# Cross attention in quarters of the context, with a running maximum

## The chip, the cores and the metric

One Trainium2 chip, one of its cores. The time is the device time of one execution in microseconds (us), median of several runs.

## The reference, cut to what matters

`x` is 8 batches of 128 tokens by 512, `ctx_768` 8 batches of 2048 context rows by 384. Everything is float32.

```python
x = x + xattn(layernorm(x), ctx_768)      # 8 heads of 64: this part is changed
x = x + attn(layernorm(x))                # causal, 128 tokens, softmax over the queries' axis
x = x + ffn(layernorm(x))                 # hidden 2048, 8-bit rounding of hidden and w2

def xattn(x, context):
    q, k, v = heads(x @ Wq), heads(context @ Wk), heads(context @ Wv)
    attn = softmax(einsum('bihd,bjhd->bhij', q, k) * 64 ** -0.5)      # over 2048 context rows
    return einsum('bhij,bjhd->bihd', attn, v) @ Wo + bo
```

## The kernel before, in words

**Split operands.** Almost every product is made of float16 halves: a value is kept as `_h` (its float16 rounding) and `_l` (the float16 of what is left), and `three_passes` (L653 to L659) multiplies high by high, low by high and high by low over the chunks of the contraction (three chunks of 128 for the context).

**Slots.** The cross attention is a loop of 128 slots (`SLOTS`). A slot is one batch, one pair of heads (4 pairs) and one quarter of the context (512 rows). Before, the order is batch, pair, quarter: four slots in a row are one pair's quarters, a stage; the context of a whole batch is held, and two batches of it (`ctx_h`, `ctx_l`). In a slot TensorE (`steady`, L808) makes
- the values of the next slot (`value_tiles`): two row tiles by four heads, 18 products of 256 columns into bank `v_ps`;
- the keys of the pair and quarter (`key_quarter`): 9 products of 512 columns into `k_ps`;
- the weighted values of five slots ago (`weighted_values`, L749 and L752): 16 products of 128 and 64 columns;
- in even slots, the scores of the last two slots (`scores`, L727), 12 products into `e_ps0` and `e_ps1`.

**The other engines** follow in an order that is written out by hand, and wait on semaphores. An engine takes its instructions in this order only, so what waits holds up all behind it.
- ScalarE (`steady`, L1238): in odd slots `quarter_bias` for two slots (the maximum as a bias), `exps` (each head's exponentials twice, as float16 `p_h` and float32 `p_f`, which also give the sums `p_sum`), `v_high` and `k_high` (the high halves out of PSUM), and once a quarter `ctx_high` with the DMA of a later quarter into `raw`.
- VectorE (`steady`, L1605): in odd slots two `quarter_maximum` (L1531), then `accumulate` (the weighted values onto `acc`, times a `fade` that brings the four quarters to one maximum), then `fade_sums`, `add_sums` or `o_reciprocal`, then `v_low`, `stage_low` once in four slots, and `k_low`. `value_tiles` waits for the `v_low` of the tile before it (`v_split`), as there is one bank.
- GpSimd (L2057): `p_low` (L1984, 1024 elements a partition), `o_norm` (four small instructions that turn `acc` into float16 halves), `ctx_low` (L1974, 1536 elements), and near the end `add_bias` and `weight_high` (L2044), with VectorE's `weight_low` behind it.
- SP's queue turns `p_h` and `p_l` by DMA transposes, then finished outputs and weights.

Before, `ctx_low` stands once in four slots, in slot 4n+2, behind `p_low`.

## Time and profile before

| | |
|---|---|
| time, median of 3 runs | 918.98 us (918.54 to 919.09) |
| span of the profiled execution, first to last instruction | 917.6 us |
| TensorE busy | 903.4 us |
| VectorE, ScalarE, GpSimd busy | 590.5, 628.3, 504.8 us |
| granted TensorE clock | full, in all 40 slices |

The profiled execution's own time is not listed beside its span; the median of the runs stands 1.4 us above that span. TensorE's matmuls overlap, so the mean duration of one is longer than its share of the time: what one costs is read from how far a group moves the start of the next. Overlap is also why a group of rows can sum to more than the time it took.

### The profile page before, as it was taken

Reading aid. Unit: us, or ns where it says so; the run is one execution under the profiler, and the core shown is the slowest. Engines: PE = TensorE matmul, PEld = TensorE weight load, DVE = VectorE, ACT = ScalarE, POOL = GpSimd, SP = SyncE. Lnnn points to the kernel's source line nnn. Section 1 sums busy time; section 2 is a strip of 40 time slices with the busy share of each in tenths; the row PEclk is TensorE's granted clock in tenths of the full one; section 3 lists DMA queues with packets and bytes.
Section 4 is the critical chain, followed back from the end, with each engine's and each line's share of the span. In section 5 each row is a group of like instructions: output and inputs, shape, how many; then the busy total and the mean of one; then the engine's idle time right before and its main releaser. Section 6 shows DMA issues by size and latency. Waiting matters only on the chain.

```text
span 917.6 us, 20100 instructions
## 1 busy us (share of the span) xinstructions
PE 903.4 (98%) x7470; PEld 564.5 (62%) x7470; DVE 590.5 (64%) x1069; ACT 628.3 (68%) x1398; POOL 504.8 (55%) x393
## 2 busy tenths in 40 slices
PE   6999999999999999999999999999999999999998
PEld 3556666666666666666666666666666455544444
DVE  6546666656666666666666666666667769886634
ACT  4857887777788788788878778877776523235540
POOL 4637656566556666666665655787777755310000
PEclk9999999999999999999999999999999999999999
DMA  9478677876767677677677868967999662333502
GB/s 333 98 142 167 135 129 141 163 145 139 136 142 131 135 146 138 132 137 141 134 143 152 157 130 140 194 133 146 186 190 165 105 133 64 72 86 74 183 13 80
DMA packets 340271, 126.38 MB, mean 138 GB/s; under 512 B 316113, under 2 KB 317905, under 8 KB 340177
## 3 DMA queue, kind: packets, MB, share of 16 engines
q1 hardware_dynamic: 325232, 96.66, 57.0%
q10 hardware_dynamic: 14944, 28.45, 9.6%
q8 instruction: 61, 1.00, 0.4%
q14 instruction: 34, 0.27, 0.1%
HBM read 45.36 MB, written 2.10 MB: 52 GB/s over the span
## 4 chain that ended last, share of the span: by engine, by line
PE 90%; DVE 3%; ACT 2%; SPq 2%; DMA 1%; issue 1%; ACTq 0%; DVEq 0%
PE v_ps L658 28%; PE k_ps L658 26%; PE e_ps L727 9%; PE e_ps L658 8%; PE o_ps L749 6%; PE o_ps L752 3%; PE e_ps L1014 3%; PE o_ps L1007 1%; PE e_ps L1007 1%; PE o_ps L768 1%; DMA raw<-in_ctx_t 1%; PE o_ps L947 1%; PE v_ps L1007 1%; DVE q_max L1531 1%; SPq L624 1%
## 5 line engine op out<-in xcount | busy, mean ns | idle before, releaser
L1984 POOL TENSOR_TENSOR p_l<-p_f,p_h 128x1024 f16<-128x1024 f32 x128 | 272.4, 2128 | 237.3 <-ACT p_f L1195 237.3
L1190 ACT ACTIVATE p_h<-e_ps,bias 128x512 f16<-128x512 f32 x256 | 175.7, 686 | 2.6 <-issue 0.5
L1195 ACT ACTIVATE p_f<-e_ps,bias 128x512 f32<-128x512 f32 x256 | 176.4, 689 | 0.0
L1526 DVE TENSOR_TENSOR k_l<-k_ps,k_h 128x512 f16<-128x512 f32 x128 | 88.5, 691 | 132.3 <-ACT k_h L1160 132.3
L1518 DVE TENSOR_TENSOR v<-v_ps,v 128x512 f16<-128x512 f32 x127 | 87.5, 689 | 107.0 <-ACT v L1152 107.0
L1531 DVE TENSOR_REDUCE q_max<-e_ps 128x2 f32<-128x1024 f32 x128 | 150.8, 1219 | 8.0 <-PE e_ps L727 0.9
L658 PE MATMUL v_ps<-wv_h,ctx_h 128*128 128x256 f16 x756 | 124.4, 273 | 1.2 <-DVE v L1518 1.1
L658 PE MATMUL v_ps<-wv_l,ctx_h 128*128 128x256 f16 x756 | 123.7, 273 | 0.0
L658 PE MATMUL v_ps<-wv_h,ctx_l 128*128 128x256 f16 x756 | 123.7, 273 | 0.0
L749 PE MATMUL o_ps<-v,pt_h 128*128 128x128 f16 x1024 | 104.2, 220 | 0.5 <-issue 0.5
L658 PE MATMUL k_ps<-ctx_h,wk_h 128*128 128x512 f16 x384 | 103.8, 379 | 0.0
L658 PE MATMUL k_ps<-ctx_h,wk_l 128*128 128x512 f16 x384 | 103.8, 379 | 0.0
L658 PE MATMUL k_ps<-ctx_l,wk_h 128*128 128x512 f16 x384 | 103.8, 379 | 0.0
L1152 ACT ACTIVATE v<-v_ps 128x512 f16<-128x512 f32 x127 | 75.6, 595 | 38.9 <-PE v_ps L658 37.4
L752 PE MATMUL o_ps<-v,pt_l 128*128 128x64 f16 x1024 | 100.8, 193 | 0.0
L1974 POOL TENSOR_TENSOR ctx_l<-raw,ctx_h 128x1536 f16<-128x1536 f32 x31 | 96.2, 3104 | 8.1 <-ACT ctx_h L1139 8.1
L749 PEld LDWEIGHTS o_ps<-v,pt_h 128*128 128x128 f16 x1024 | 90.3, 98 | 15.7 <-issue 0.9
L752 PEld LDWEIGHTS o_ps<-v,pt_l 128*128 128x128 f16 x1024 | 88.6, 98 | 14.9
L1166 ACT ACTIVATE bias<-q_max 128x2 f32<-128x2 f32 x128 | 26.1, 204 | 93.0 <-DVE q_max L1531 93.0
L658 PEld LDWEIGHTS v_ps<-wv_h,ctx_h 128*128 128x128 f16 x756 | 64.6, 98 | 34.4 <-issue 27.6
L1160 ACT ACTIVATE k_h<-k_ps 128x512 f16<-128x512 f32 x128 | 76.5, 598 | 6.8 <-PE k_ps L658 0.7
L658 PEld LDWEIGHTS v_ps<-wv_h,ctx_l 128*128 128x128 f16 x756 | 74.0, 98 | 8.6
(311 smaller groups left out, 1399.0 us busy)
## 6 DMA issues: line engine op xcount, KB each, us to landing
raw<-in_ctx_t ACTq DMA_DIRECT2D x26, 768.0 KB, 5.3
w_raw<-in_w_t SPq DMA_DIRECT2D x32, 256.0 KB, 3.8
raw<-in_ctx_t SPq DMA_DIRECT2D x5, 768.0 KB, 7.0
pt_h<-p_h SPq DMA_TRANSPOSE x128, 3.7
pt_l<-p_l SPq DMA_TRANSPOSE x128, 3.3
out<-xr SPq DMA_DIRECT2D x7, 256.0 KB, 2.0
x_in<-in_x SPq DMA_DIRECT2D x6, 256.0 KB, 11.0
o_all<-in_x ACTq DMA_DIRECT2D x6, 256.0 KB, 3.5
```

The costliest lines, as they stand in the source:

```text
L658: mm = pe.matmul(acc, a(c), m(c), start=(i == 0), stop=(i == len(todo) - 1))
L727: mm = pe.matmul(e_ps[s % 2][:, h, :], left[rows, p, tokens], right[rows, n % 2, cols], start=first, stop=last)
L749: pe.matmul(acc_bank[:, h * VW:h * VW + VW], pt_h[:, s % T_RING, h * JT + j, :], v[g][:, tile, 2 * (p % 2) + h, :], start=(j == 0 and h == ...
L752: mm = pe.matmul(acc_bank[:, h * VW:h * VW + DH], pt_l[:, s % T_RING, h * JT + j, :], v[g][:, tile, 2 * (p % 2) + h, 0:DH], start=False, s ...
L1160: act.activation(k_h[:, n % 2, q * QW:q * QW + QW], k_ps[:, :], ACT.Copy).then_inc(k_hi, 1)
L1190: act.activation(p_h[:, s % H_RING, h, :], e_ps[s % 2][:, h, :], ACT.Exp, scale=EXP_SCALE, bias=bias[:, n % 2, h, q:q + 1]).then_inc(p_hi, 1)
L1195: act.activation(p_f[:, s % F_RING, h, :], e_ps[s % 2][:, h, :], ACT.Exp, scale=EXP_SCALE, bias=bias[:, n % 2, h, q:q + 1], accum_out=p_su ...
L1518: dve.tensor_tensor(v[g][:, j0:j0 + 2, :, DH:VW], v_bank(s)[:, :].rearrange("p (j h d) -> p j h d", j=2, d=DH), v[g][:, j0:j0 + 2, :, 0:DH ...
L1526: dve.tensor_tensor(k_l[:, n % 2, cols], k_ps[:, :], k_h[:, n % 2, cols], ALU.subtract).then_inc(k_split, 1)
L1531: dve.tensor_reduce(q_max[:, s % 2, :], e_ps[s % 2][:, :, :], AX, ALU.max, negate=True).then_inc(e_maxed, 1)
L1974: pool.tensor_tensor(ctx_l[b % 2][:, q, :, :], raw[:, i % 2, :, :], ctx_h[b % 2][:, q, :, :], ALU.subtract).then_inc(ctx_split, 1)
L1984: pool.tensor_tensor(p_l[:, s % L_RING, :, :], p_f[:, s % F_RING, :, :], p_h[:, s % H_RING, :, :], ALU.subtract).then_inc(p_split, 1)
```

## The change

The loop's order becomes batch, quarter, pair. A unit is one quarter of one batch: four slots, one for each pair of heads.
- A unit's context is used up in its four slots, so the context is held for two units and not two batches; keys, values and weights' staging have short rings of their own (`K_RING`, `V_RING`, `W_RING`).
- From unit 1 on, `value_tiles` makes one row tile for all eight heads: 9 products of 512 columns a slot.
- The maximum is a running one: from a batch's second quarter on, `q_max` goes through a `min` with the `run` of the quarter before (the maxima are kept negated), and `run` makes the bias. `gaps` and `fades_of` make the factor by which `acc` is faded before a quarter is added.
- The sums of the exponentials come out of the weighted values: each head's values have a column of ones, so their products are 129 and 65 columns wide. `accum_out`, `fade_sums` and `add_sums` go.
- `ctx_high` and `ctx_low` of quarter i stand in slot 4i-4. All pairs of a batch end in its last four slots, and `o_norm` with them. The weights' split begins two slots earlier.
- At the start, `wv_low(1)`, `wk_low(1)` and `wk_low(2)` stand around `row_stats`, and the contexts' loads are later.

```diff
-VW = 2 * DH
+VW = 2 * DH + 2
+SUM_AT = 2 * DH
...
 F_RING, H_RING, L_RING, T_RING = 2, 3, 2, 3
-EARLY_CTX = 6
+K_RING, V_RING, W_RING = 4, 3, 4
...
+        FIRST_SPLIT = SLOTS - 18
+
...
+        GAPS = [s for s in range(0, SLOTS, 2) if s // PAIRS % QUARTERS]
+
+        def gaps_at(s):
+            return GAPS.index(s)
 
...
-        ctx_behind = {0: 2, 1: 3, 5: 4}
-        load_behind = {6: EARLY_CTX}
-        for n in range(1, STAGES):
-            if QUARTERS + n < B * QUARTERS:
-                ctx_behind[QUARTERS * n + 2] = QUARTERS + n
-            if EARLY_CTX + n < B * QUARTERS:
-                load_behind[QUARTERS * n + 3] = EARLY_CTX + n
+        ctx_behind = {1: 1}
+        load_behind = {}
+        for i in range(2, UNITS):
+            ctx_behind[PAIRS * i - 4] = i
+        for i in range(3, UNITS):
+            load_behind[PAIRS * i - 9] = i
...
 
-            load_ctx(1)
+            load_wv(1)
             for r in range(4, B):
                 sp.dma_start(x_in[:, r, :], x[r]).then_inc(x_landed[r], 16)
-            load_wv(1)
+            load_ctx(1)
             for row, src in ((bo_row, xbo), (bv_row, abv), (b2_row, b2)):
                 sp.dma_start(row[:, :], src.rearrange("(a n) -> a n", a=1).broadcast_to([P, D]))\
...
-                ch, cl = ctx_h[b % 2], ctx_l[b % 2]
-                cols = wv_cols(g)
-                for j in (j0, j0 + 1):
-                    rows = slice(j % JT * P, j % JT * P + P)
-                    half = (j - j0) * 256
-                    mm = three_passes(v_bank(s)[:, half:half + 256],
-                                      (lambda c: ch[:, j // JT, c, rows], lambda c: cl[:, j // JT, c, rows]),
-                                      (lambda c: wv_h[:, c, cols], lambda c: wv_l[:, c, cols]), CC)
+                if i == 0:
+                    for j in (2 * (t % 2), 2 * (t % 2) + 1):
+                        rows, half, cols = slice(j * P, j * P + P), j % 2 * 256, wv_cols(t // 2)
+                        mm = three_passes(v_bank(s)[:, half:half + 256],
+                                          (lambda c: ctx_h[:, 0, c, rows], lambda c: ctx_l[:, 0, c, rows]),
+                                          (lambda c: wv_h[:, c, cols], lambda c: wv_l[:, c, cols]), CC)
+                else:
+                    rows = slice(t * P, t * P + P)
+                    mm = three_passes(v_bank(s)[:, :],
+                                      (lambda c: ctx_h[:, i % 2, c, rows], lambda c: ctx_l[:, i % 2, c, rows]),
+                                      (lambda c: wv_h[:, c, :], lambda c: wv_l[:, c, :]), CC)
                 mm.then_inc(v_filled, 1)
 
...
+                    pe.wait_ge(v_ones, 1)
                     pe.wait_ge(q_split, 8)
                 acc_bank = o_ps[s % 2]
                 for h in range(2):
+                    at = h * VW
                     for j in range(JT):
-                        tile = q * JT + j
-                        pe.matmul(acc_bank[:, h * VW:h * VW + VW], pt_h[:, s % T_RING, h * JT + j, :],
-                                  v[g][:, tile, 2 * (p % 2) + h, :],
+                        pe.matmul(acc_bank[:, at:at + SUM_AT + 1], pt_h[:, s % T_RING, h * JT + j, :],
+                                  v[:, i % V_RING, j, 2 * p + h, 0:SUM_AT + 1],
                                   start=(j == 0 and h == 0), stop=False, skip_group_check=True)
-                        mm = pe.matmul(acc_bank[:, h * VW:h * VW + DH], pt_l[:, s % T_RING, h * JT + j, :],
-                                       v[g][:, tile, 2 * (p % 2) + h, 0:DH],
+                        mm = pe.matmul(acc_bank[:, at + DH:at + SUM_AT + 1], pt_l[:, s % T_RING, h * JT + j, :],
+                                       v[:, i % V_RING, j, 2 * p + h, DH:SUM_AT + 1],
                                        start=False, stop=(j == JT - 1), skip_group_check=True)
...
-                    act.wait_ge(q_filled, 8)
-                act.activation(ctx_h[b % 2][:, q, :, :], raw[:, i % 2, :, :], ACT.Copy).then_inc(ctx_hi, 1)
+                if i >= 2:
+                    act.wait_ge(v_filled, PAIRS * (i - 1))
+                    act.wait_ge(k_filled, PAIRS * (i - 1))
+                act.activation(ctx_h[:, i % 2, :, :], raw[:, i % 2, :, :], ACT.Copy).then_inc(ctx_hi, 1)
...
                 act.wait_ge(k_filled, s + 1)
-                if n >= 2:
-                    act.wait_ge(e_filled, s - 7)
-                act.activation(k_h[:, n % 2, q * QW:q * QW + QW], k_ps[:, :], ACT.Copy).then_inc(k_hi, 1)
+                if s >= K_RING:
+                    act.wait_ge(e_filled, s - K_RING + 1)
+                act.activation(k_h[:, s % K_RING, :], k_ps[:, :], ACT.Copy).then_inc(k_hi, 1)
 
...
+            def fades_of(s):
+
+                i, p = unit_of(s)
+                act.wait_ge(gap_ready, gaps_at(s) + 1)
+                if i >= 2:
+                    act.wait_ge(acc_ready, s - 2 * PAIRS + 2)
+                act.activation(fade[:, i % 2, p:p + 2, :], gap[:, i % 2, p:p + 2, :], ACT.Exp, scale=EXP_SCALE)\
+                    .then_inc(fade_ready, 1)
 
...
                 act.activation(p_h[:, s % H_RING, h, :], e_ps[s % 2][:, h, :], ACT.Exp, scale=EXP_SCALE,
-                               bias=bias[:, n % 2, h, q:q + 1]).then_inc(p_hi, 1)
-                if n >= 2 and q == 0 and h == 0:
-
-                    act.wait_ge(o_rec_ready, 3 * (n - 2) + 1)
+                               bias=bias[:, i % 2, p, h:h + 1]).then_inc(p_hi, 1)
                 act.activation(p_f[:, s % F_RING, h, :], e_ps[s % 2][:, h, :], ACT.Exp, scale=EXP_SCALE,
-                               bias=bias[:, n % 2, h, q:q + 1], accum_out=p_sum[:, n % 2, h, q:q + 1]).then_inc(p_full, 1)
+                               bias=bias[:, i % 2, p, h:h + 1]).then_inc(p_full, 1)
 
             first_ctx_high(0)
...
             wk_high(slice(P, D))
-            ctx_high(1)
-            ctx_high(2)
+            wv_high(1)
             for i in range(3):
                 q_high(i)
...
             def quarter_maximum(s):
 
+                i, p = unit_of(s)
                 dve.wait_ge(e_filled, s + 1)
-                dve.tensor_reduce(q_max[:, s % 2, :], e_ps[s % 2][:, :, :], AX, ALU.max, negate=True).then_inc(e_maxed, 1)
-
-            def stage_low(n):
-
-                dve.wait_ge(bias_ready, 4 * n + 4)
-                dve.tensor_reduce(low[:, n % 2, :, :], bias[:, n % 2, :, :], AX, ALU.min).then_inc(low_ready, 1)
+                if i >= 2:
+                    dve.wait_ge(bias_ready, s - 2 * PAIRS + 1)
+                if i % QUARTERS == 0:
+                    dve.tensor_reduce(run[:, i % 2, p, :], e_ps[s % 2][:, :, :], AX, ALU.max, negate=True).then_inc(e_maxed, 1)
+                    return
+                dve.tensor_reduce(q_max[:, s % 2, :], e_ps[s % 2][:, :, :], AX, ALU.max, negate=True).then_inc(q_maxed, 1)
+                dve.wait_ge(q_maxed, PAIRS * (i - 1 - i // QUARTERS) + p + 1)
+                dve.wait_ge(e_maxed, s - PAIRS + 1)
+                dve.tensor_tensor(run[:, i % 2, p, :], q_max[:, s % 2, :], run[:, 1 - i % 2, p, :], ALU.min).then_inc(e_maxed, 1)
+
+            def gaps(s):
+
+                i, p = unit_of(s)
+                dve.wait_ge(e_maxed, s + 2)
+                if gaps_at(s) >= 4:
+                    dve.wait_ge(fade_ready, gaps_at(s) - 3)
+                dve.tensor_tensor(gap[:, i % 2, p:p + 2, :], run[:, i % 2, p:p + 2, :], run[:, 1 - i % 2, p:p + 2, :],
+                                  ALU.subtract).then_inc(gap_ready, 1)
 
...
             def accumulate(s):
 
-                n, q = stage_of(s)
+                i, p = unit_of(s)
+                b, q = quarter_of(i)
                 dve.wait_ge(pv_done, s + 1)
                 if q == 0:
-                    dve.wait_ge(fade_ready, n + 1)
-                    if n >= 2:
-                        dve.wait_ge(o_ready, n - 1)
-                else:
-                    dve.wait_ge(acc_ready, s)
+                    if b:
+                        dve.wait_ge(o_ready, PAIRS * (b - 1) + p + 1)
+                    dve.tensor_copy(acc[:, p, :, 0:SUM_AT + 1],
+                                    o_ps[s % 2][:, 0:2 * VW].rearrange("p (h n) -> p h n", h=2)[:, :, 0:SUM_AT + 1])\
+                        .then_inc(acc_ready, 1)
+                    return
+                dve.wait_ge(fade_ready, gaps_at(s - s % 2) + 1)
+                dve.wait_ge(acc_ready, s - PAIRS + 1)
                 for h in range(2):
-                    new, total = o_ps[s % 2][:, h * VW:h * VW + VW], acc[:, n % 2, h, :]
-                    faded = fade[:, n % 2, h, q:q + 1]
-                    if q == 0:
-                        ins = dve.tensor_scalar(total, new, faded, None, ALU.mult)
-                    else:
-                        ins = dve.scalar_tensor_tensor(total, new, faded, total, ALU.mult, ALU.add)
+                    total = acc[:, p, h, 0:SUM_AT + 1]
+                    ins = dve.scalar_tensor_tensor(total, total, fade[:, i % 2, p, h:h + 1],
+                                                   o_ps[s % 2][:, h * VW:h * VW + SUM_AT + 1], ALU.mult, ALU.add)
                 ins.then_inc(acc_ready, 1)
 
...
+            def o_reciprocal(s):
+
+                i, p = unit_of(s)
+                b = i // QUARTERS
+                dve.wait_ge(acc_ready, s + 1)
+                if b:
+                    dve.wait_ge(o_ready, PAIRS * (b - 1) + p + 1)
+                dve.reciprocal(o_rec[:, p, :, :], acc[:, p, :, SUM_AT:SUM_AT + 1]).then_inc(o_rec_ready, 1)
 
...
                 turned_low_x(r)
+            wv_low(1)
+            wk_low(1)
             row_stats(x_groups[2])
+            wk_low(2)
             for i in range(4):
                 q_low(i)
 
...
                 if 0 <= done < SLOTS:
                     accumulate(done)
-                    if done % QUARTERS:
-                        (fade_sums, add_sums, o_reciprocal)[done % QUARTERS - 1](done // QUARTERS)
+                    if done // PAIRS % QUARTERS == QUARTERS - 1:
+                        o_reciprocal(done)
                 if 0 < s and s + 1 < SLOTS:
                     v_low(s + 1)
                 if 0 <= s - FIRST_SPLIT - 1 < 16:
                     weight_low(s - FIRST_SPLIT - 1)
-                if 0 <= s - X_LAG < SLOTS and (s - X_LAG) % QUARTERS == 2:
-                    stage_low((s - X_LAG) // QUARTERS)
+                if s - X_LAG in GAPS:
+                    gaps(s - X_LAG)
                 if 0 < s < SLOTS:
                     k_low(s)
 
...
+            pool.memset(v[:, :, :, :, SUM_AT:SUM_AT + 1].rearrange("p a j h n -> p (a j h) n"), 1.0).then_inc(v_ones, 1)
...
-                n, q = stage_of(s)
                 if s >= X_LAG:
                     p_low(s - X_LAG)
-                if s >= FIRST_SPLIT and s % 2 == 0:
+                if 0 <= s - FIRST_SPLIT < 16 and s % 2 == 0:
                     weight_high(s - FIRST_SPLIT)
                     weight_high(s - FIRST_SPLIT + 1)
                 done = s - PV_LAG - 1
-                if done >= 0 and done % QUARTERS == 3:
-                    o_norm(done // QUARTERS)
+                if done >= 0 and done // PAIRS % QUARTERS == QUARTERS - 1:
+                    o_norm(done // (PAIRS * QUARTERS) * PAIRS + done % PAIRS)
...
                 pool.tensor_tensor(xr[:, r, :], xr[:, r, :], o_all[:, r, :], ALU.add).then_inc(x1n_ready, 1)
 
             p_low(SLOTS - 3)
-            o_norm(STAGES - 2)
             p_low(SLOTS - 2)
...
 
             for r in range(3):
                 inverse_deviation(r)
+                o_norm(STAGES - 4 + r)
             for r in range(3):
                 norm_low(1, r)
             o_norm(STAGES - 1)
```

## Rows read from the trace of the kernel before

**Rows 1.** The page: busy us, share of the span and instructions of each engine.

```profile
PE 903.4 (98%) x7470; PEld 564.5 (62%) x7470; DVE 590.5 (64%) x1069; ACT 628.3 (68%) x1398; POOL 504.8 (55%) x393
```

**Rows 2.** The chain, one pair of slots and the next one's start: start us, us, what.

```profile
560.16 2.07 PE v_ps L658 x18
562.23 1.94 PE k_ps L658 x9
564.85 1.97 PE v_ps L658 x18
...
570.84 2.07 PE v_ps L658 x18
```

**Rows 3.** Timeline of a pair with `ctx_low`: start us, us, engine, line, operation, tiles.

```profile
217.72 2.35 DVE L1531 TENSOR_REDUCE q_max<-e_ps 128x2 f32<-128x1024 f32 x2
...
218.26 0.50 PE L658 MATMUL v_ps<-wv_h,ctx_h 128*128 128x256 f16 x3
218.34 3.10 POOL L1974 TENSOR_TENSOR ctx_l<-raw,ctx_h 128x1536 f16<-128x1536 f32 x1
...
218.98 0.20 ACT L1166 ACTIVATE bias<-q_max 128x2 f32<-128x2 f32 x1 [0.73 <-DVE q_max L1531]
...
220.51 0.96 DVE L1563 TENSOR_TENSOR p_faded<-p_sum,fade 128x8 f32<-128x8 f32 x1
220.56 0.59 ACT L1152 ACTIVATE v<-v_ps 128x512 f16<-128x512 f32 x1
...
221.39 0.68 DVE L1518 TENSOR_TENSOR v<-v_ps,v 128x512 f16<-128x512 f32 x1
...
222.47 2.13 POOL L1984 TENSOR_TENSOR p_l<-p_f,p_h 128x1024 f16<-128x1024 f32 x1 [1.02 <-ACT p_f L1195]
...
222.85 0.38 PE L658 MATMUL v_ps<-wv_h,ctx_h 128*128 128x256 f16 x2
```

**Rows 4.** `p_faded` alone: the whole span, then 300 to 600 us; shortest, median, longest.

```profile
L1563 DVE TENSOR_TENSOR p_faded<-p_sum,fade x32: 156/961/2189, 71.1 to 729.1; 128x8 f32<-128x8 f32 x32
...
L1563 DVE TENSOR_TENSOR p_faded<-p_sum,fade x14: 956/962/971, 306.0 to 583.7; 128x8 f32<-128x8 f32 x14
```

**Rows 5.** Timeline of a pair in which `add_bias` comes before `ctx_low`.

```profile
604.13 3.10 POOL L1974 TENSOR_TENSOR ctx_l<-raw,ctx_h 128x1536 f16<-128x1536 f32 x1
...
605.07 2.19 DVE L1563 TENSOR_TENSOR p_faded<-p_sum,fade 128x8 f32<-128x8 f32 x1
...
607.19 2.13 POOL L1984 TENSOR_TENSOR p_l<-p_f,p_h 128x1024 f16<-128x1024 f32 x1
...
608.00 0.49 PE L658 MATMUL v_ps<-wv_h,ctx_h 128*128 128x256 f16 x3 [0.42 <-DVE v L1518]
```

**Rows 6.** Timeline of GpSimd: the two `weight_high` of a pair.

```profile
646.93 3.06 POOL L2044 TENSOR_SCALAR av_h<-raw 128x512 f16<-128x512 f32 x2
```

**Rows 7.** Timeline of VectorE and TensorE at the start.

```profile
32.15 0.49 PE L658 MATMUL v_ps<-wv_h,ctx_h 128*128 128x256 f16 x3 [0.20 <-DVE v L1518]
...
6.07 0.96 DVE L1494 SCALAR_TENSOR_TENSOR wv_l<-wv_raw,wv_h 128x768 f16<-128x768 f32 x1
...
22.70 2.46 DVE L1466 BATCH_NORM_STATS2 stats<-x_in 128x6 f32<-128x512 f32 x4
...
33.23 0.55 DVE L1500 SCALAR_TENSOR_TENSOR wk_l<-wk_raw,wk_h 128x384 f16<-128x384 f32 x1
```

**Rows 8.** Timeline of GpSimd, TensorE and SP's queue behind the loop.

```profile
747.34 1.03 PE L658 MATMUL e_ps<-wo_h,q_h 128*128 128x512 f16 x4
...
731.94 2.28 POOL L2089 TENSOR_TENSOR n_half<-o_all,n_half 128x512 f16<-128x512 f32 x2
...
738.83 0.45 POOL L1990 TENSOR_TENSOR o_sum<-acc 128x128 f32<-128x128 f32 x1 [2.43 <-DVE o_rec L1574]
...
740.59 0.22 POOL L1962 TENSOR_SCALAR rstd<-mean_var 128x1 f32<-128x1 f32 x1
...
740.95 1.26 SPq L558 DMA_TRANSPOSE q_h<-o_half  x1
```

243 lines of the change are left out of this document (100 added, 143 removed).

## Prediction

> **What bounds the kernel now.** I read the page first, then the chain of waits, then the timeline of one pair of slots on all engines, and last the slowest forms on VectorE. The page says that TensorE is busy for 903.4 of 917.6 us [rows 1]; no other engine reaches 70%. In the chain, one pair of slots (odd, then even) of the cross attention repeats without a gap: values 1.97, keys 1.94, the weighted values 0.68, the three again, and the 1.40 that are left before the next pair's values for two sets of scores, 10.68 us in all (560.16 to 570.84) [rows 2]. So TensorE streams columns from one end of the loop to the other, and the change can gain only by fewer columns or fewer bubbles, and lose by any new bubble. The granted clock is full throughout. What stands beside TensorE is a relay: scores end, VectorE takes two maxima, ScalarE makes a bias and the exponentials, and between them ScalarE and VectorE copy the value bank out in two halves (`v_high`, `v_low`), which TensorE needs back before its next values. One such pair begins at 218.26 [rows 3]; `v_low` could have begun at 221.15, when `v_high` is done, and TensorE wants the bank at 222.85. That is some 1.0 us of slack, and it is what the change has to live in.
>
> **The products.** Values: 18 products of 256 columns take 1.97 us, 9 of 512 (the key products) take 1.94 [rows 2]. So 109 ns for 256 columns and 216 for 512: the price is by column, and halving the count gives 0.03 us a slot. Unit 0 keeps the old form, so 124 slots: -3.7 us. Weighted values: 16 products a slot, each one column wider (128 to 129, 64 to 65). At 216/512 = 0.42 ns a column that is 6.7 ns a slot, +0.9 us over 128 slots. No row shows an odd count; the lower bound is that 0.9, the upper one that a 65- or 129-column product costs some 10 ns more (a quarter of its 0.68/16 = 42 ns), +20 us. The columns still lie next to each other, so I take the lower one.
>
> The Trainium skill (TensorE: Matmul & The Clock Gate, Back-to-back issue gap) gives about 131 ns for 512 columns in a sustained stream, and N/2.4 + 2.5 ns for a single one. The key rows agree with the second and not with the first; by the first, the values would fall to 1.18 us a slot and the change would win some 98 us.
>
> **What VectorE gets.** Removed: `fade_sums`, `add_sums` and `stage_low`, each once in four slots. Added: in 96 of 128 slots (all but the first quarter of a batch) a `tensor_tensor` min of `q_max` with the earlier `run`, 128x2, between the maximum and the bias, and in 48 slots one `gap`. `p_faded` is the same kind of instruction, tiny and with both inputs in SBUF. Alone it takes 156 ns; but its median is 961, and between 300 and 600 us all 14 take 956 to 971 [rows 4]. The timeline shows why [rows 3]: it starts at 220.51 and ends at 221.47, and GpSimd's `ctx_l` subtraction runs from 218.34 to 221.44. Another pair shows it again [rows 5]: `ctx_l` from 604.13 to 607.23, `p_faded` from 605.07 to 607.26. GpSimd has its next instruction ready at 607.19, and VectorE still gets through. So such an instruction waits until GpSimd's current one is over. The reduction from PSUM is not held: both maxima run beside `ctx_l` [rows 3].
>
> The Trainium skill says the same (SBUF — State Buffer, Who interferes with whom): a VectorE instruction with two SBUF inputs contends with a GpSimd one that reads SBUF, and the later fully blocks. It speaks against this change; the sum below rests on the rows alone.
>
> **Where the new minimum lands.** Before, `p_faded` met `ctx_l` late, behind all that mattered. The new minimum is issued right after the first maximum, at about T+0.7 us (T is the pair's first value product; the bias started at 218.98, T+0.72). `ctx_l` then runs from T+0.08 to T+3.18 [rows 3]. The change keeps it there: `ctx_behind` puts quarter i in slot 4i-4, an even one, behind ScalarE's `ctx_high`, so it starts as before with the next pair. The relay then reads: min ends T+3.2, bias T+3.3. From there to the end of `v_high` the rows have 2.17 us (218.98 to 221.15), less some 0.1 since the sums no longer come out of the exponentials: T+5.4. Second maximum and second minimum (1.2 + 0.2 after T+3.2) are ready at T+4.6, when the second bias needs them. `v_low` takes 0.69: T+6.1. TensorE wanted the bank at 222.85, T+4.59, now T+4.56. With 0.06 for the semaphore it waits 1.6 us. Behind `v_low` on VectorE stand `gap` and `k_low`; `k_h` is written at about T+7.0 and TensorE wants the keys at T+8.1, so nothing more is lost. The next pair has no `ctx_l` beside it and starts clean.
>
> How often: `ctx_l` of quarters 2 to 31, 30 times, is followed by the maxima of unit i-2. Eight of those units (0, 4, ... 28) are a batch's first quarter, with no minimum. 22 are left, 20 before the weights' work starts: 20 x 1.6 = +32 us. Bounds for one: 0 if the minimum gets in before `ctx_l`, and 2.5 (3.2 - 0.7) if the relay has no slack at all. I take 1.6, since every step has its row.
>
> In pairs without `ctx_l`, GpSimd's `p_l` of the pair before ends at about T+0.1, the minimum runs free, and the bias comes 0.2 us later: inside the 1.0 of slack, 0. `gap` comes behind `v_low`, at about T+3.7, and `p_l` starts at T+4.2 [rows 3]: 0.5 us of room, 0.
>
> From slot 110 on GpSimd also does `weight_high`, two of 1.5 us a pair [rows 6], before `ctx_l`. The first holds the minimum only to T+1.6, and `ctx_l` now falls on `gap`: I take +1.5 us for six pairs together (0 to 10).
>
> The two stalls of 0.42 us where `p_faded` met a late `ctx_l` ([rows 5], and the same once more 22 us later) go: -0.8.
>
> **Start and end.** `ctx_high(1)`, `ctx_high(2)` and their waits leave ScalarE's start, but TensorE hardly waited for them: its own wait is 0.20 [rows 7]. In their stead VectorE does `wv_low(1)` (0.96) and two `wk_low` (0.55 each) around `row_stats`, which stood at 22.70 [rows 7], and on that hang the norms, `x_high`, `v_high(2)` and `v_low(2)`, for which TensorE stood at 32.15. 2.1 us later, less the 0.3 or so that the earlier `q_high` gives: +1.7 (0 to 3).
>
> At the end all four head pairs of the last batch close together. GpSimd has three `o_norm` of 1.8 us (738.83 to 740.59) between `rstd` and `norm_low`, where it had some 5 us of idle time, 2.43 of it before `o_sum` [rows 8]. `norm_low(0..2)`, which began at 731.94, moves back by about 3.5, and with it six transposes of 1.3 us on SP's queue and the last output's two behind them (the first of these was issued at 740.95 and took 1.26). `project_out(7)` needs these at 747.34, and they land at about 748.5: +1.2 (0 to 4).
>
> **Sum.** -3.7 + 0.9 + 32 + 1.5 - 0.8 + 1.7 + 1.2 = +32.8. On the span of 917.6 that is 950.4; the median of the runs is 1.4 above that span, so about 951.5.
>
> **Rivals.**
> (a) The lock is not met, or ends harmlessly (the minimum passes before `ctx_l`, or GpSimd's start slips behind it): without 32 and 1.5 the span changes by -0.7, a time of 918.3. For it: `ctx_l` leads the minimum by only 0.6 us. Against it: it keeps that lead, since both start from the end of the same keys.
> (b) Faster: the same, and neither start nor end costs its 1.7 and 1.2: 915.4. It decides if no minimum is held and VectorE's earlier splits hide behind `turned_low_x`.
> (c) `gap` is late by half a microsecond, meets `p_l` (2.13 us) and holds `k_low` in the other pairs too: `k_low` ends at T+6.9 where T+6.5 was wanted, 0.4 in some 40 pairs: +16, 968.
> (d) Odd widths cost 10 ns a product: +20, 971.
> (e) A 512-column product costs less by the column than the key rows show. If it took no more than a 256-column one (109 ns), the values would cost 0.98 us a slot, 119 less in all than forecast: 832. The key products already have that width and show 216 ns. (The page on TensorE named above would put it at 131 ns, and the time at 857.)
>
> **Chances.** The forecast 0.79, (a) 0.07, (b) 0.05, (c) 0.06, (d) 0.02, (e) 0.01. The likeliest's own range comes from 1.2 to 2.1 us a stall: 942 to 962. The whole range keeps that and some of (c) and of a milder lock: 938 to 964. A difference under 0.2% (1.8 us) can't be told from none. Faster is (b) and (e), 0.06; same (a), 0.07; slower 0.87.
>
> **What would show it.** In the changed kernel's trace: `run` minima of 160 ns and, 20 to 22 of them, some 2.5 us long, ending with `ctx_l`; as many waits of TensorE for `v_low`, 1.6 us each; value products 1.94 us a slot; pairs that alternate between about 10.6 and 12.2 us, all of 10.6 where the maxima are a first quarter's. The prediction is wrong if the minima are all short, `gap` is long in most pairs, or the weighted values take more than 0.70 us a slot.

## The result, and the profile of the changed kernel

The changed kernel takes 967.3 us (965.1 to 968.0) where the kernel before takes 918.8 (918.5 to 919.1): a ratio of 1.052 (1.050 to 1.053), slower. The forecast was 951.5 in a range of 938 to 964. The sign and the mechanism came as forecast, the time is 3 us outside the range, and 15.4 us of the 48.2 by which the span grew (965.8 against 917.6) are not in my sum.

The busy times of the page, and the granted clock in its 40 slices:

```profile
PE 912.1 (94%) x6354; PEld 459.8 (48%) x6354; DVE 642.5 (67%) x1085; ACT 596.9 (62%) x1126; POOL 508.6 (53%) x394
...
PEclk9999999999999999999999999999899999999999
```

TensorE does 6354 products where it did 7470 [rows 1]: nine of 512 columns take the place of eighteen of 256 in 124 slots, 1116 fewer. It is idle for nearly 6% of the span, where it was for under 2%. The waits of TensorE, with the sum, the count and the longest:

```profile
PE v_ps L679 <- DVE v L1517: 30.5, 24, 1.5
PE k_ps L679 <- DVE k_l L1521: 8.7, 3, 3.6
...
PE o_ps L769 <- DMA pt_l<-p_l: 2.0, 1, 2.0
PE v_ps L679 <- DVE f_l L1668: 1.2, 1, 1.2
PE e_ps L679 <- DMA q_l<-o_half: 0.7, 1, 0.7
```

The first line is the forecast one, a wait for `v_low`: 18 of the 24 lie between slots 8 and 104 and last 1.39 or 1.40 us each. The second was not forecast: three waits for `k_low`. One pair of slots with `ctx_low`, all engines, from the timeline:

```profile
306.37 0.82 PE L679 MATMUL v_ps<-wv_h,ctx_h 128*128 128x512 f16 x3
...
306.42 3.10 POOL L1971 TENSOR_TENSOR ctx_l<-raw,ctx_h 128x1536 f16<-128x1536 f32 x1
...
307.09 2.45 DVE L1535 TENSOR_TENSOR run<-q_max,run 128x2 f32<-128x2 f32 x1
...
309.57 0.20 ACT L1176 ACTIVATE bias<-run 128x2 f32<-128x2 f32 x1 [3.22 <-DVE run L1535]
...
311.05 0.60 ACT L1164 ACTIVATE v<-v_ps 128x512 f16<-128x512 f32 x1
...
311.68 0.69 DVE L1517 TENSOR_TENSOR v<-v_ps,v 128x512 f16<-128x512 f32 x1 [0.26 <-ACT v L1164]
312.29 0.15 DVE L1543 TENSOR_TENSOR gap<-run 128x4 f32<-128x4 f32 x1
312.52 0.81 PE L679 MATMUL v_ps<-wv_h,ctx_h 128*128 128x512 f16 x3 [1.40 <-DVE v L1517]
```

This is the pair of [rows 3] with the minimum in it. With T = 306.37, the minimum starts at T+0.72 and ends with `ctx_l` at T+3.17 (forecast T+3.2), `v_high` ends at T+5.28 (5.4), `v_low` at T+6.0 (6.1), and TensorE has waited 1.40 us (1.6). From the chain of waits, such a pair is 12.2 us long (its first value product at 306.37, the next pair's at 318.59), and the one behind it, without `ctx_low`, 10.67 (318.66 to 329.33 in the chain). All durations of the two new instructions (shortest, median, longest, in ns):

```profile
L1535 DVE TENSOR_TENSOR run<-q_max,run x96: 160/161/2446, 70.6 to 767.6; 128x2 f32<-128x2 f32 x96
L1543 DVE TENSOR_TENSOR gap<-run x48: 152/152/2078, 73.5 to 768.2; 128x4 f32<-128x4 f32 x48
```

19 of the 96 minima take over 2 us: 18 end with `ctx_l`, between slots 8 and 104 (20 to 22 were forecast), and the one at 709.32 ends with a `p_l`. `gap` is short (under 0.3 us) in 41 of 48 pairs.

**Where the 48.2 us lie.** I compare the start of every slot's key products in the two traces. This table gives how much later a slot's keys start than before (us):

| slot | 0 | 2 | 8 | 16 | 24 | 104 | 110 | 112 | 114 | 116 | 120 | 122 | 124 | 127 | end of span |
|---|---|---|---|---|---|---|---|---|---|---|---|---|---|---|---|
| later by | -0.2 | 1.3 | 1.1 | 4.2 | 5.7 | 28.5 | 31.5 | 32.6 | 36.4 | 39.2 | 40.3 | 44.1 | 45.6 | 45.6 | 48.2 |

Start 1.1; slots 8 to 104, 18 steps of 1.55 less the cheaper products, 27.4; slots 104 to 127, with `add_bias` and then the weights' split, 17.1; behind the loop 2.6. My sum had 1.7, 26.6, 3.3 and 1.2 there. (26.6 is 18 of the twenty stalls, 28.8, less 2.2 for the products; 3.3 is the other two, 3.2, and the 1.5 for the weights' slots, less the 0.8 of the old stalls and 0.6 for the products.) So the miss is in the third part.

Its first 3.0 us, slots 104 to 110, come before any weight is split. GpSimd's `add_bias` stands ahead of `ctx_l` there, so a minimum takes 1.3 us at most, and `ctx_l` meets `gap` instead:

```profile
644.65 3.71 POOL L2025 TENSOR_TENSOR o_all<-o_all,bo_row 128x512 f32<-128x512 f32 x3
648.32 3.09 POOL L1971 TENSOR_TENSOR ctx_l<-raw,ctx_h 128x1536 f16<-128x1536 f32 x1
```

```profile
647.10 1.28 DVE L1535 TENSOR_TENSOR run<-q_max,run 128x2 f32<-128x2 f32 x1
...
649.75 1.69 DVE L1543 TENSOR_TENSOR gap<-run 128x4 f32<-128x4 f32 x1
```

TensorE waits 0.55, 0.68 and 1.41 us for `v_low` in these slots, which comes near the 3.2 us of the two whole stalls that I had put here, by another way. The miss lies behind slot 110.

What happens in the weights' slots, from 110 on, on VectorE and GpSimd (the timeline of each) and on TensorE:

```profile
669.50 3.06 POOL L2040 TENSOR_SCALAR av_h<-w_in 128x512 f16<-128x512 f32 x2
672.63 3.10 POOL L1971 TENSOR_TENSOR ctx_l<-raw,ctx_h 128x1536 f16<-128x1536 f32 x1
675.69 2.57 POOL L1981 TENSOR_TENSOR p_l<-p_f,p_h 128x1024 f16<-128x1024 f32 x1
```

```profile
671.29 0.40 DVE L1535 TENSOR_TENSOR run<-q_max,run 128x2 f32<-128x2 f32 x1
...
673.05 3.23 DVE L1580 SCALAR_TENSOR_TENSOR av_l<-w_in,av_h 128x512 f16<-128x512 f32 x1
676.20 2.07 DVE L1543 TENSOR_TENSOR gap<-run 128x4 f32<-128x4 f32 x1
678.20 0.68 DVE L1521 TENSOR_TENSOR k_l<-k_ps,k_h 128x512 f16<-128x512 f32 x1
```

```profile
674.57 0.81 PE L679 MATMUL v_ps<-wv_l,ctx_h 128*128 128x512 f16 x3
679.02 1.44 PE L679 MATMUL k_ps<-ctx_h,wk_h 128*128 128x512 f16 x3 [3.64 <-DVE k_l L1521]
680.26 1.49 PE L679 MATMUL k_ps<-ctx_h,wk_l 128*128 128x512 f16 x3
681.54 1.49 PE L679 MATMUL k_ps<-ctx_l,wk_h 128*128 128x512 f16 x3
682.82 0.32 PE L769 MATMUL o_ps<-v,pt_h 128*128 128x129 f16 x1
```

`weight_high` does shield the minimum, as I wrote (0.40 us). But `ctx_l` then runs beside `weight_low`, which takes 3.23 us instead of 0.69, and the `p_l` behind it holds `gap` for 2.07. Both stand ahead of `k_low` on VectorE, and TensorE waits 3.64 us for it. Behind that wait the keys take 3.80 us (679.02 to 682.82) instead of 1.94 at a full clock [rows 2]. The windows show the granted clock of that stretch:

```profile
675.00:700.00 25.00, 21.36 (x135) 10.23 (x134) 17.84 (x29) 15.15 (x29) 18.86 (x18) 0.86 0.85 177
...
725.00:750.00 25.00, 21.38 (x147) 10.18 (x146) 19.01 (x31) 14.44 (x30) 16.01 (x9) 0.93 0.81 163
```

The columns behind the length are the busy times of PE, PEld, DVE, ACT and POOL, then the granted clock, the DMA share and GB/s. The nine key products at 3.80 us are 422 ns for 512 columns, that is the lower level, 1.2 GHz. The same happens once more, with a wait of 3.62 us at 729.40. The steps 112 to 116 (6.6 us) and 120 to 124 (5.3 us) are these two.

### The profile page after: what moved, and what is told of

Read it like the earlier page. It is cut to its first block, busy times and chain, and to the rows that moved or that the text cites. A ratio compares the mean times of both kernels' runs of the same rounds, so it can differ in the third digit from the quotient of the medians.

```text
span 965.8 us, 17868 instructions
## 1 busy us (share of the span) xinstructions
PE 912.1 (94%) x6354; PEld 459.8 (48%) x6354; DVE 642.5 (67%) x1085; ACT 596.9 (62%) x1126; POOL 508.6 (53%) x394
## 4 chain that ended last, share of the span: by engine, by line
PE 71%; DVE 13%; ACT 7%; issue 3%; POOL 1%; SPq 1%; DMA 1%; ACTq 0%; DVEq 0%; POOLq 0%
PE v_ps L679 21%; PE k_ps L679 20%; PE e_ps L748 7%; PE e_ps L679 7%; DVE run L1535 5%; PE o_ps L769 4%; DVE q_max L1532 4%; PE e_ps L1034 3%; PE o_ps L772 2%; ACT p_h L1199 2%; ACT v L1164 2%; PE o_ps L1027 2%; DVE v L1517 2%; PE e_ps L1027 1%; ACT p_f L1201 1%
## 5 line engine op out<-in xcount | busy, mean ns | idle before, releaser
L679 PE MATMUL v_ps<-wv_h,ctx_h 128*128 128x512 f16 (+1 forms) x384 | 103.0, 377 | 30.5 <-DVE v L1517 30.5
L1532 DVE TENSOR_REDUCE q_max<-e_ps 128x2 f32<-128x1024 f32 x96 | 117.2, 1221 | 7.8 <-PE e_ps L748 2.1
L1176 ACT ACTIVATE bias<-run 128x2 f32<-128x2 f32 x128 | 26.0, 203 | 150.6 <-DVE run L1535 127.7
L769 PE MATMUL o_ps<-v,pt_h 128*128 128x129 f16 x1024 | 106.8, 221 | 2.0 <-DMA pt_l<-p_l 2.0
L772 PE MATMUL o_ps<-v,pt_l 128*128 128x65 f16 x1024 | 103.4, 193 | 0.0
L1971 POOL TENSOR_TENSOR ctx_l<-raw,ctx_h 128x1536 f16<-128x1536 f32 x31 | 96.0, 3098 | 12.3 <-ACT ctx_h L1156 11.7
L679 PE MATMUL v_ps<-wv_l,ctx_h 128*128 128x512 f16 (+1 forms) x384 | 102.5, 376 | 0.0
L679 PE MATMUL v_ps<-wv_h,ctx_l 128*128 128x512 f16 (+1 forms) x384 | 102.5, 376 | 0.0
L772 PEld LDWEIGHTS o_ps<-v,pt_l 128*128 128x128 f16 x1024 | 90.8, 98 | 15.1 <-issue 0.3
L1535 DVE TENSOR_TENSOR run<-q_max,run 128x2 f32<-128x2 f32 x96 | 65.6, 683 | 3.3
L679 PEld LDWEIGHTS v_ps<-wv_h,ctx_h 128*128 128x128 f16 x384 | 28.2, 97 | 75.4 <-issue 60.1
```

The costliest lines, as they stand in the source:

```text
L679: mm = pe.matmul(acc, a(c), m(c), start=(i == 0), stop=(i == len(todo) - 1))
L769: pe.matmul(acc_bank[:, at:at + SUM_AT + 1], pt_h[:, s % T_RING, h * JT + j, :], v[:, i % V_RING, j, 2 * p + h, 0:SUM_AT + 1], start=(j == ...
L772: mm = pe.matmul(acc_bank[:, at + DH:at + SUM_AT + 1], pt_l[:, s % T_RING, h * JT + j, :], v[:, i % V_RING, j, 2 * p + h, DH:SUM_AT + 1], ...
L1532: dve.tensor_reduce(q_max[:, s % 2, :], e_ps[s % 2][:, :, :], AX, ALU.max, negate=True).then_inc(q_maxed, 1)
L1535: dve.tensor_tensor(run[:, i % 2, p, :], q_max[:, s % 2, :], run[:, 1 - i % 2, p, :], ALU.min).then_inc(e_maxed, 1)
L1971: pool.tensor_tensor(ctx_l[:, i % 2, :, :], raw[:, i % 2, :, :], ctx_h[:, i % 2, :, :], ALU.subtract).then_inc(ctx_split, 1)
```

## The experiments

My theory: GpSimd's `ctx_low` holds a VectorE instruction with two SBUF inputs (the lock), and what stands behind it is late. Rivals: the minimum, or the whole new order, costs by itself; the sum of GpSimd's work counts and not who holds whom; products of odd widths cost more. "Later by" is always the start of a slot's keys against the kernel before. The kernel before ran beside each of them, at 918.6 to 919.1.

### e1: without the minimum

```diff
-                dve.tensor_reduce(q_max[:, s % 2, :], e_ps[s % 2][:, :, :], AX, ALU.max, negate=True).then_inc(q_maxed, 1)
...
-                dve.tensor_tensor(run[:, i % 2, p, :], q_max[:, s % 2, :], run[:, 1 - i % 2, p, :], ALU.min).then_inc(e_maxed, 1)
+                dve.tensor_reduce(run[:, i % 2, p, :], e_ps[s % 2][:, :, :], AX, ALU.max, negate=True).then_inc(e_maxed, 1)
```

Each quarter is scaled by its own maximum; `gap` and `fade` still bring `acc` along, so the result for these inputs is the same but for rounding. What goes is a bound: with a running maximum the fade is never above 1, while here it grows as the exponential of the drop when a quarter's maximum lies below the one before. The same holds for all runs below without the minimum.

> The changed kernel without the running minimum: each quarter's own maximum goes straight into run, and the fade (which is then the factor between two quarters' maxima) keeps the sum exact. Theory (the lock: the minimum's two SBUF inputs wait for GpSimd's ctx_l): the 18 waits of TensorE for v_low, 1.4 us each before slot 104, are gone, so 966.6 falls by 28, and by 0 to 5 more in the weights' slots, where gap and weight_low still meet ctx_l: 933 to 939. Rival (the order and the short rings themselves make the pair longer): the waits stay, at 960 or more.

926.9 us (924.5 to 929.4), ratio 1.009 (1.007 to 1.011): 40 us less than with the minimum. Between slots 8 and 104 there is no wait for `v_low` (one of 0.26 us comes before slot 8), and the slots drift from +0.5 to -0.1. In slots 104 to 127 6.3 us are still lost, with three waits for `k_low` (3.9 in all) and three ahead of the weighted values (4.0). So the minimum makes all of the steady loss and most, but not all, of the loss in the weights' slots. That is 6 us below the least that I expected (933), since the weights' slots lose 10.8 less as well.

### e2: the minimum in another form

```diff
-                dve.tensor_tensor(run[:, i % 2, p, :], q_max[:, s % 2, :], run[:, 1 - i % 2, p, :], ALU.min).then_inc(e_maxed, 1)
+                for h in range(2):
+                    ins = dve.tensor_scalar(run[:, i % 2, p, h:h + 1], q_max[:, s % 2, h:h + 1],
+                                            run[:, 1 - i % 2, p, h:h + 1], None, ALU.min)
+                ins.then_inc(e_maxed, 1)
```

> The minimum stays, but run comes in as a pointer scalar (two tensor_scalar of 128x1 a slot in place of one tensor_tensor of 128x2), so there is one SBUF tensor input. Theory (two tensor inputs are what is held): no long minima, some 0.2 us a slot more on VectorE, inside the slack: 934 to 941. Rival (any VectorE instruction that reads run and q_max in SBUF is held, or the chain through one more dependent instruction is what costs): 960 or more.

932.2 us (931.2 to 933.3), ratio 1.014 (1.013 to 1.016), 2 us below what I expected. The old `run` comes in as a scalar read by address, so there is one tensor input. Beside the same `ctx_low`:

```profile
L1536 DVE TENSOR_SCALAR run<-q_max,run x192: 203/209/216, 69.8 to 732.4; 128x1 f32<-128x1 f32 x192
```

None of 192 is held, though all do the same work from the same place on the engine, twice the instructions. The slots stand at -0.3 in slot 104. This tells the lock from the minimum's length: up to slot 104 the running maximum costs nothing; its form does. The weights' slots still lose 11.7 us, with waits for `k_low` of 3.65 and 3.64.

### e3: a minimum in the kernel before

```diff
-                dve.tensor_reduce(q_max[:, s % 2, :], e_ps[s % 2][:, :, :], AX, ALU.max, negate=True).then_inc(e_maxed, 1)
+                dve.tensor_reduce(q_raw[:, s % 2, :], e_ps[s % 2][:, :, :], AX, ALU.max, negate=True).then_inc(e_maxed, 1)
+                dve.wait_ge(e_maxed, 2 * s + 1)
+                dve.tensor_tensor(q_max[:, s % 2, :], q_raw[:, s % 2, :], q_raw[:, s % 2, :], ALU.min).then_inc(e_maxed, 1)
```

> The kernel before, with one tensor_tensor more: the maximum goes through a minimum with itself (128x2, both inputs in SBUF) before the bias; nothing else of the change. Theory (the lock at this place is enough): each of the 27 pairs with ctx_l from slot 6 on gains a wait of 1.4 to 1.6 us, +38 to +43 less the 0.8 of p_faded's own stalls: 955 to 962. Rival (the minimum costs only its 0.16 us, or only together with the new order): 919 to 924.

968.3 us (967.8 to 969.1), ratio 1.054 (1.052 to 1.055). A minimum of a number with itself, 160 ns long and without any use, costs the old order as much as the whole change costs:

```profile
PE v_ps L658 <- DVE v L1518: 43.2, 30, 2.4
```

```profile
L1533 DVE TENSOR_TENSOR q_max<-q_raw x128: 160/161/2987, 38.7 to 768.4; 128x2 f32<-128x2 f32 x128
```

So the steady loss needs nothing of the new order. It is 6 us more than the most that I expected (962): each of the 30 contexts now meets a minimum (a batch's first quarter has one too), and a step is 1.68 us (40.3 us over the 24 of slots 8 to 104).

### e4: values in 256 columns again

```diff
-                    rows = slice(t * P, t * P + P)
-                    mm = three_passes(v_bank(s)[:, :],
...
+                for j in (2 * (t % 2), 2 * (t % 2) + 1):
+                    rows, half, cols = slice(j * P, j * P + P), j % 2 * 256, wv_cols(t // 2)
+                    mm = three_passes(v_bank(s)[:, half:half + 256],
```

> The changed kernel with its values in 256-column products in all units (two row tiles by four heads, 18 a slot), nothing else. Theory (the price is by column): the value group takes 1.97 in place of 1.94 us, 124 times: 966.6 + 3 to 4 = 970, less where TensorE waits anyway. Rival (512 columns are cheaper by the piece, hidden under the stalls): 980 or more. If 512 columns bring nothing: 966 to 968.

969.5 us (969.0 to 969.9), 2.2 more than the changed kernel. Over slots 8 to 104 it loses 1.84 us more, 19 ns a slot. So half as many products of twice the columns gain 19 ns of 1.95 us, 2.4 us in all; my term was 30 ns and 3.7 us. From a value group's start to that of the keys behind it the two traces differ by 22 ns; the 19 are less, I take it, because in the 18 stalled pairs one of the two gains falls into the wait. Without stalls it would be some 2.7 us (my estimate, 124 times 22 ns). The price is by the column, and rival (e) falls.

### e5 and e6: the weights' slots without the held instructions

e5 is e1 with `gap` taken out as well (first cut), e6 also moves `weight_low` behind `k_low` (second):

```diff
-                act.activation(fade[:, i % 2, p:p + 2, :], gap[:, i % 2, p:p + 2, :], ACT.Exp, scale=EXP_SCALE)\
...
+                for t in (p, p + 1):
+                    for h in range(2):
+                        ins = act.activation(fade[:, i % 2, t, h:h + 1], bias[:, 1 - i % 2, t, h:h + 1], ACT.Exp,
+                                             scale=-1.0, bias=bias[:, i % 2, t, h:h + 1])
...
-                if s - X_LAG in GAPS:
-                    gaps(s - X_LAG)
```

```diff
-                if 0 <= s - FIRST_SPLIT - 1 < 16:
-                    weight_low(s - FIRST_SPLIT - 1)
                 if 0 < s < SLOTS:
                     k_low(s)
+                if 0 <= s - FIRST_SPLIT - 1 < 16:
+                    weight_low(s - FIRST_SPLIT - 1)
```

> The changed kernel without the running minimum and without the gap subtractions as well (the fade is taken by ScalarE as an exponential of the difference of the two biases, four small activations a pair of slots; the result is the same up to rounding). Without the minimum the loss left was 7.8 us, 6.2 of it in the weights' slots. My theory: there GpSimd holds two VectorE instructions that stand ahead of k_low, gap and weight_low. Without gap only weight_low is left: 922 to 926, TensorE's waits for k_low in those slots fewer but not gone. Rival: what is late there is GpSimd's own work (p_low, weight_high and ctx_low back to back), whatever VectorE does: then the time stays at 926 to 928.

> As the kernel without minimum and gap, with weight_low issued behind k_low on VectorE instead of ahead of it. My theory: no held instruction stands ahead of k_low any more, so TensorE's waits for k_low go: 918.5 to 922, what is left being start and end (2 to 3 us), less the values' gain. Rival (GpSimd's own work is the limit): the same as the kernel without the gap, within 1 us.

e5 924.3 us (922.8 to 928.5), e6 926.5 (925.7 to 927.4). e5 is inside what I expected, e6 is not: the waits for `k_low` went (none is left), but 5.5 us are still lost between slots 104 and 127, now as waits ahead of the weighted values (4.4) and for `v_low`. GpSimd's groups of e6 from 618 to 700 us:

```profile
L1976 POOL TENSOR_TENSOR p_l<-p_f,p_h 128x1024 f16<-128x1024 f32 x15 | 33.9, 2268 | 4.3 <-DMA pt_l<-p_l 3.1 <-ACT p_f L1204 1.1
L2035 POOL TENSOR_SCALAR av_h<-w_in 128x512 f16<-128x512 f32 x8 | 12.6, 1572 | 0.7
L1966 POOL TENSOR_TENSOR ctx_l<-raw,ctx_h 128x1536 f16<-128x1536 f32 x4 | 12.4, 3098 | 0.2
L2035 POOL TENSOR_SCALAR wo_h<-w_in 128x512 f16<-128x512 f32 x6 | 9.3, 1542 | 0.5
```

Ahead of `p_l` it waits for 4.3 us in 82, and 3.1 of these for a ring of its own output to be turned by the DMA. I read this as GpSimd being full, so that `p_l` is late, and with it the transposes and the weighted values. The trace itself names no releaser for these waits of TensorE, and the 3.1 us would also fit a late queue of transposes; e14 and e15 below test it.

### e7: the changed kernel with weight_low behind k_low, alone

The move of the second cut above, and nothing else: the minimum and `gap` stay.

> The changed kernel, minimum and gap kept, with only weight_low moved behind k_low. The changed kernel loses 17.1 us between slots 104 and 126, of which my prediction had some 5.5. My theory: the 3.6 us waits of TensorE for k_low are weight_low held by ctx_low, and with gap alone ahead of k_low a wait is at most about 1.5; the granted clock then stays full. 957 to 962 (5 to 10 less than the changed kernel's 967). Rival: the loss there comes from the minimum or from gap, and stays: 965 to 968.

959.6 us (959.1 to 960.1), 7.7 less than the changed kernel, as expected. The clock is full to the end, and slots 104 to 127 cost 9.8 us instead of 17.1. Of TensorE's waits from 610 to 755 us, the one for `k_low`, which was 3.6 us at its longest:

```profile
PE k_ps L679 <- DVE k_l L1521: 0.9, 2, 0.4
```

### e8: ctx_low one slot earlier

```diff
-            ctx_behind[PAIRS * i - 4] = i
+            ctx_behind[PAIRS * i - 5] = i
```

> The changed kernel with GpSimd's ctx_low (and ScalarE's ctx_high with it) one slot earlier, so that it starts in the middle of a pair, about 6.3 us after the pair's first value product, and is over when the next pair's minimum is issued. Nothing is taken out. My theory (the min costs only where it meets ctx_low): the steady part's 18 waits of 1.4 us go, 28 us: 930 to 940, and below that if the weights' slots gain too. Rival (the min lengthens the relay by itself, or it then meets p_low in every pair): 955 or more.

930.4 us (929.6 to 932.0), ratio 1.013 (1.011 to 1.014). One digit gives back 37 of the 48 us, with nothing taken out. Slots 8 to 104 drift by 0.1 us in all, and slots 104 to 127 still lose 7.1. Its minima:

```profile
L1535 DVE TENSOR_TENSOR run<-q_max,run x96: 160/160/1571, 71.1 to 730.5; 128x2 f32<-128x2 f32 x96
```

Not one of them takes over 2 us.

### e9, e10 and e12: weight_high on VectorE

e9 is e6 with `weight_high` moved from GpSimd to VectorE, just ahead of `weight_low`. e10 is e9 with the start's order changed (`row_stats`, three `q_low`, `wk_low(1)`, `wv_low(1)`, `q_low(3)`, `wk_low(2)`). e12 has the same moves, e8's, and the order of e16 (below) at the end, with minimum and gap kept. The cut is e9's:

```diff
                 if 0 <= s - FIRST_SPLIT - 1 < 16:
+                    weight_high(s - FIRST_SPLIT - 1)
                     weight_low(s - FIRST_SPLIT - 1)
```

> The kernel without minimum and gap and with weight_low behind k_low (926.5), with weight_high issued by VectorE just ahead of weight_low instead of by GpSimd. In that kernel GpSimd is idle for under 5 of the 82 us from 618 to 700 us of the span, and TensorE waits for p_l's transposes. My theory now: since ctx_low goes on beside the weights' work and four o_norm fall together, GpSimd itself is full there. 3.1 us a pair taken off it: the 5.5 us between slots 104 and 126 fall to 0 to 1.5, time 920 to 922.5. Rival: VectorE, with 1.1 us a pair more, becomes late itself, or p_l is late for another reason (the transposes on SP's queue): 925 or more.

> The kernel before this one in the list (weight_high on VectorE), with row_stats(x_groups[2]) at the start ahead of wv_low(1) and the two wk_low, which then stand around q_low(3). My prediction put 1.7 us (0 to 3) on that order. If it is right, the first slots begin 1.0 to 1.7 us earlier and the time falls as much, to 918.5 to 921. Rival (the loss at the start comes from ScalarE's order or from later loads): no change, within 0.5 us.

> The changed kernel with all of the change kept, minimum and gap too, and only its order mended: ctx_low one slot earlier (930.4 alone), weight_low behind k_low and weight_high on VectorE, row_stats first at the start, and at the end norm_low(1, 0) and (1, 1) ahead of the third o_norm. Theory: the values' gain less the odd widths is about 0.6 us, all stalls but a few of gap and the minimum against ctx_low in the weights' slots go: 918.5 to 922. Rival (with minimum and gap there is no order without a held instruction ahead of k_low): 925 or more.

e9 935.4 us (935.0 to 936.5), e10 935.9 (935.4 to 937.1), e12 936.3 (935.6 to 939.1): all three outside what I expected, and `weight_high` on VectorE is in all three. VectorE in e9:

```profile
636.21 1.06 DVE L1578 TENSOR_SCALAR av_h<-w_in 128x512 f16<-128x512 f32 x1
637.30 3.47 DVE L1586 SCALAR_TENSOR_TENSOR av_l<-w_in,av_h 128x512 f16<-128x512 f32 x1
640.69 2.34 DVE L1532 TENSOR_REDUCE run<-e_ps 128x2 f32<-128x1024 f32 x2
```

`weight_high` pushes `weight_low` past the start of `ctx_l` (637.01 to 640.21). `weight_low` then takes 3.47 us, to 640.77, now ahead of the next pair's maxima, and TensorE waits 3.17 us for `v_low` at 644.89. I had priced the move by its 1.1 us of work and not by what it would meet: the mistake of the prediction once more. e10 can't tell of the start, since TensorE then waited 1.93 us at 29.07 for `wv_low(1)`, which I had put too late. In e12 the longest wait for `v_low`, 3.92 us at 671.46, has `weight_high` (2.03 us) and `weight_low` (2.50) ahead of the maxima as well. So e12 doesn't settle whether the change can be mended with minimum and gap kept; e2's form of the minimum was not tried in a mended order.

### e11: narrower weighted values

```diff
-                        pe.matmul(acc_bank[:, at:at + SUM_AT + 1], pt_h[:, s % T_RING, h * JT + j, :],
+                        less = int(j > 0)
+                        pe.matmul(acc_bank[:, at:at + SUM_AT + 1 - less], pt_h[:, s % T_RING, h * JT + j, :],
```

(On top of e1. The products with `pt_l` likewise; three of four row tiles are left out of the sums.)

> The changed kernel without the minimum (926.9), with the weighted values' products 128 and 64 columns wide for three of the four row tiles, so that the sums hold only a quarter of the exponentials (that part is left out). 12 of 16 products a slot have even widths again. By the column alone the group of 16 products takes 5 ns less, 0.6 us in all; by the slots' steps of the changed kernel (a slot's 0.70 against 0.68) it takes 15 ns less, 1.9 us in all. Rival of the prediction (10 ns a product): 15 us less. So 925 to 926.3 by my theory.

924.3 us (923.6 to 924.8), where e1 has 926.9; I expected 925 to 926.3. Over slots 8 to 104 e1 drifts by -0.59 us and this by -1.65: 11 ns a slot for twelve products, 0.9 ns each, where the column alone is 0.42. For all sixteen that is 15 ns a slot and 1.9 us, my term was 7 ns and 0.9. Rival (d), 10 ns a product, falls.

### e13 and e14: ctx_low short beside the weights' work

```diff
-                pool.tensor_tensor(ctx_l[:, i % 2, :, :], raw[:, i % 2, :, :], ctx_h[:, i % 2, :, :],
+                n = QW // 4 if i >= 29 else QW
+                pool.tensor_tensor(ctx_l[:, i % 2, :, 0:n], raw[:, i % 2, :, 0:n], ctx_h[:, i % 2, :, 0:n],
```

e13 does this to the changed kernel, e14 to e6. Three quarters of the low halves of three units, 29 to 31, are left out.

> The changed kernel with ctx_low of units 29, 30 and 31 (those issued beside the weights' work, in slots 112, 116 and 120) cut to a quarter of its columns, so that it lasts some 0.8 us instead of 3.1 (the rest of those low halves is left out). Nothing else moves. My theory: the two waits of TensorE of 3.6 us, and the lower granted clock behind them, come from weight_low held by ctx_low and gap held by the p_low behind it: both go, 9 to 12 us less: 955 to 959. Rival (weight_high and p_low hold them as well, or GpSimd's sum of work counts and not which instruction is long): at most 3 us less, 964 or more.

> The kernel without minimum and gap and with weight_low behind k_low (926.5), with ctx_low of units 29 to 31 cut to a quarter in the same way. No held instruction stands ahead of k_low there, so what this takes away is GpSimd's time, 7 us of the 82 in which it was idle for under 5. My theory (GpSimd is full): 2.5 to 5.5 us less, 921 to 924. Rival (the wait is for SP's queue of transposes, or VectorE's): 925.5 or more.

e13 958.2 us (957.2 to 960.0), e14 923.5 (923.1 to 924.1): both as expected. In e13 slots 104 to 127 cost 8.5 us instead of 17.1, the longest wait for `k_low` is 1.5, and the clock is full. So `ctx_low`'s length in three slots alone, 112, 116 and 120, makes half of the loss there. The other half is still waits for VectorE, from 610 to 755 us:

```profile
PE v_ps L679 <- DVE v L1517: 4.3, 4, 1.6
PE k_ps L679 <- DVE k_l L1521: 3.7, 3, 1.5
```

In e14, which has no held instruction ahead of `k_low`, 7 us less of GpSimd's work takes 3.0 us off. The waits ahead of the weighted values fall from 4.4 to 1.4 us, those for `v_low` stay (0.4 and 0.9): GpSimd's sum of work counts there, as I read e6.

### e15 to e18: mended step by step

e15 is e6 with `weight_high` on ScalarE, behind `ctx_high` (first cut). e16 adds the two ends (second):

```diff
+                if 0 <= s - FIRST_SPLIT < 16 and s % 2 == 0:
+                    weight_high(s - FIRST_SPLIT)
+                    weight_high(s - FIRST_SPLIT + 1)
```

```diff
-            wv_low(1)
-            wk_low(1)
             row_stats(x_groups[2])
-            wk_low(2)
-            for i in range(4):
+            wv_low(1)
+            for i in range(3):
                 q_low(i)
+            wk_low(1)
+            q_low(3)
+            wk_low(2)
...
-            for r in range(3):
-                inverse_deviation(r)
-                o_norm(STAGES - 4 + r)
-            for r in range(3):
-                norm_low(1, r)
+            inverse_deviation(0)
+            o_norm(STAGES - 4)
+            inverse_deviation(1)
+            inverse_deviation(2)
+            o_norm(STAGES - 3)
+            norm_low(1, 0)
+            norm_low(1, 1)
+            o_norm(STAGES - 2)
+            norm_low(1, 2)
```

> The same kernel (926.5) with weight_high on ScalarE, behind ctx_high in even slots, where it was idle for 3.7 us before the next pair's bias. Takes 3.1 us a pair off GpSimd without putting a held instruction between k_low and the maxima. Theory: slots 104 to 126 cost 0 to 1.5 instead of 5.5, 920.5 to 923. Rival (ScalarE becomes late, or weight_low behind k_low still meets ctx_low and delays the maxima, as on VectorE): 925 or more.

> The kernel with weight_high on ScalarE, with the two ends mended too: at the start row_stats, then wv_low(1), the first three q_low, wk_low(1), q_low(3), wk_low(2); at the end norm_low(1, 0) and (1, 1) ahead of the third o_norm. Theory by my terms: the start gives 0.7 to 1.3 and the end 0.8 to 1.3 less than the kernel with weight_high on ScalarE; a time of 918 to 921, which is the kernel before within the bound. Rival (the start's loss is the contexts' loads): only the end's gain.

e15 924.0 us (923.7 to 925.6), 1 us above what I expected: 3.0 us are still lost between slots 104 and 127, as waits of 0.3 to 0.8 for `v_low`. e16 921.3 (920.9 to 922.2). It starts slot 8 at -0.5 where e15 starts it at +0.4, so by these two traces the start's order was worth 0.8 to 0.9 of the 1.1. Single traces spread, though: those with the changed start and this `ctx_low` have slot 8 at 0.3 to 1.3, those with the mended start (e16 to e18) at -0.5 to -0.1. And behind slot 127 nothing is lost any more, where e15 loses 1.5.

e17 is e16 with both `weight_low` of a pair in the odd slot, e18 also makes the weighted values' products 130 and 66 columns wide:

```diff
-                if 0 <= s - FIRST_SPLIT - 1 < 16:
+                if 0 <= s - FIRST_SPLIT - 1 < 16 and s % 2 == 1:
                     weight_low(s - FIRST_SPLIT - 1)
+                    weight_low(s - FIRST_SPLIT)
```

```diff
-                        pe.matmul(acc_bank[:, at:at + SUM_AT + 1], pt_h[:, s % T_RING, h * JT + j, :],
+                        pe.matmul(acc_bank[:, at:at + SUM_AT + 2], pt_h[:, s % T_RING, h * JT + j, :],
```

> The mended kernel (921.3) with both weight_low of a pair in the odd slot, behind its k_low, where only the next slot's v_low follows with room; none stands ahead of the maxima any more. Theory: the waits for v_low of 0.34, 0.61, 0.80, 0.34 and 0.34 us between 650 and 710 us go, 2.4 us: 918.5 to 920, which is the kernel before within 0.2%. Rival (they come from something else, or the two held subtractions now delay the even slot's v_low): 921 or more.

> The kernel with both weight_low in the odd slot, with a second column of ones, so that the weighted values' products are 130 and 66 columns wide instead of 129 and 65 (the second sum is made and not used). By the column a slot costs 7 ns more, 0.9 us in all. If the odd count is what costs, the excess of about 8 ns a slot goes and the two cancel: the same time within 0.3 us. If it is no matter of odd or even: 0.9 us more or above.

e17 917.7 us (916.5 to 919.5), ratio 0.9985 (0.9976 to 0.9994): a little better than I expected. e18 917.3 (916.4 to 919.0), ratio 0.9983 (0.9974 to 0.9992). e15's and e16's five waits for `v_low` between 650 and 710 us are gone, and e17's slots 110 to 127 stand between -1.3 and -2.0. From e17's page and its waits of TensorE:

```profile
PE 902.1 (99%) x6354; PEld 457.2 (50%) x6354; DVE 563.0 (62%) x941; ACT 636.8 (70%) x1286; POOL 483.8 (53%) x378
```

```profile
PE v_ps L716 <- ACT ctx_h L1125: 6.6, 1, 6.6
PE v_ps L679 <- DVE v L1532: 1.0, 2, 0.8
PE o_ps L769 <- issue: 0.7, 1, 0.7
PE v_ps L788 <- ACT wq_h L1111: 0.6, 1, 0.6
```

The one long wait left, 6.6 us for the first context, stands in the kernel before as well (7.1 us).

So the new order, the short rings, the 512-column values and the column of ones, without the minimum and with the work around them in other places, take 1 to 1.5 us less than the kernel before. Both intervals lie below 1, but the gain is less than the 0.2% that I gave as the bound. It is also not the change as it was: without the running maximum nothing bounds the fade (see e1). e18 against e17: both drift by -0.59 us from slot 8 to 104, so one column more costs nothing beyond 129 and 65.

## Why the prediction was right in kind and too low in size

| term | forecast | measured | from |
|---|---|---|---|
| values in 512 columns | -3.7 | -2.4 (-2.7 without stalls) | e4 |
| weighted values one column wider | +0.9 | +1.9 | e11 |
| minimum held by `ctx_low`, slots to 104 | 18 x 1.6 = +28.8 | 18 x 1.55 = +27.9 | a pair's length, 12.22 less 10.67 |
| weights' slots, 104 to 127, products apart | +3.9 | +17.2 | table |
| start | +1.7 | +1.1 | table |
| end | +1.2 | +2.6 | table |

- **The lock.** Right in place, time and size: the minimum starts at T+0.72 and ends at T+3.17. e2 (same minimum, other form: no loss), e3 (minimum without the change: the whole loss) and e8 (minimum and `ctx_low` apart: no loss up to slot 104) show it from three sides. Rival (a), the lock not met, did not come; e8 shows the order in which it does. None of the three signs of being wrong came up to slot 104: 18 minima are long there, `gap` is short in 41 of 48 pairs, and the weighted values take 0.70 us (0.68 before). Two small things of the working were off: the 0.06 us for the semaphore came from no row and is 0.14 to 0.15 in all 24 waits, and the parts of a pair give its 10.68 us only with 2.07 for its first values [rows 2], where the text has 1.97. The Trainium skill (SBUF — State Buffer, Who interferes with whom) gives the rule by the number of SBUF inputs, not by size; e2 and e3 agree.
- **The step that failed** is "The first holds the minimum only to T+1.6, and `ctx_l` now falls on `gap`: I take +1.5 us for six pairs together (0 to 10)". The first half held: the minimum at 671.29 takes 0.40 us. In the second I named `gap` and overlooked `weight_low`, which has two SBUF inputs too and stood right where the shifted `ctx_l` starts. I also took [rows 6] for the new kernel's GpSimd, but before, `ctx_low` is over when the weights' work begins; now it goes on to slot 120 beside it. One such pair costs 3.6 us of waiting and, behind it, 1.6 or 2.8 us more by half the granted clock. The two pairs alone cost 11.9 of the 17.2 us that stand in place of my +3.9. e7 (7.7 us back) and e13 (9 us back) show that it was `weight_low` ahead of `k_low`, and `ctx_low`'s length beside it. What e13 keeps, 8.5 us, is waits of 0.6 to 1.6 us for `v_low` and `k_low`, the 3.0 before slot 110 among them; which held instruction makes each was not tested one by one. GpSimd's own load counts once these are gone (e14).
- **Products.** Both terms were mis-sized in the same direction, 2.3 us together: the 512-column products gain 19 ns a slot here and not 30, the wider ones cost 15 and not 7. The Trainium skill (TensorE: Matmul & The Clock Gate, Back-to-back issue gap) gives 131 ns for a sustained 512-column product; e4 and the 1.94 us of nine such products (216 ns each) do not agree with it.
- **Start and end.** The start's mechanism is borne out by e16 to e18, to some 1 us. At the end e16 gives back the 1.5 us that e15 loses by the order of `o_norm` and `norm_low`; the changed kernel loses 1.1 more, with a wait of 2.0 us for `pt_l` that I did not take apart. Runs with the end's order unchanged lose from 0.3 (e2) to 2.6 us (e7) behind slot 127, so the order alone does not fix that term, and its size stays open.
- **Rivals.** (c) did not come: `gap` is short (under 0.3 us) in 41 of 48 pairs. (b), (d) and (e) fell with the runs above.
- **The range.** Its upper end took the steady stall's error for the main one. The bound of "0 to 10" for the weights' slots came from no row: two held instructions in a row ahead of `k_low`, in three pairs, would have given 3 x (3.1 + 2.1) = 15.6 us less the slack (my estimate, from the durations of `ctx_l` and `p_l`), and that is where it should have been worked out.

## What to carry to other kernels

A tiny instruction is priced by what it meets and who stands behind it: 160 ns of work cost 28 us here, and the same minimum with one tensor input nothing. When a long GpSimd instruction moves, list every VectorE instruction with two SBUF inputs (and a wide `tensor_scalar` with one, see below) that it now lies beside, at the new place and for as long as it goes on, and not only the one that the change adds. Try a shift by one slot before giving a change up: it gave back 37 of 48 us.

## What the runs showed of the hardware that I had not expected

- A `tensor_scalar` whose scalar comes from SBUF by address is not held (203 to 216 ns in 192 instructions of 128x1 in e2), where the same minimum as a `tensor_tensor` is (up to 2446).
- A `tensor_scalar` of 128x512 with one SBUF input is held too: 420 ns for each of two at the start of e9, with GpSimd quiet, and 1060 to 1796 for its sixteen in the weights' slots. Each of these sixteen starts beside a `p_l` of GpSimd and ends 0.28 or 0.29 us after it. The Trainium skill (SBUF — State Buffer, Who interferes with whom) has this: such an instruction may use both of VectorE's port pairs, and then contends. The trace agrees.
- GpSimd pays as well: `p_l` takes 2.57 us and not 2.13 where VectorE's held instruction is let in (the rows from 673.05 and 675.69 above: `weight_low`, held until `ctx_l` ends, gets through to 676.28 while `p_l` has begun).
- Sixteen products of 129 and 65 columns cost 15 ns more than of 128 and 64 (from e11's twelve), and those of 130 and 66 nothing more.
- The granted clock fell to its lower level (1.2 GHz) behind both waits of 3.6 us in the changed kernel, behind one of 3.64 in e2, two of 3.62 and 3.58 in e4, one of 3.60 in e5, of 3.58 in e9 and in e10, and of 3.92 in e12. It stayed full behind one of 3.65 in e2 (646.13), of 3.17 in e9 and in e10, and of 2.85 in e6. Where it fell behind a wait for `k_low`, the slots behind took 1.4 to 2.8 us more than usual. So a wait of that length may cost this much more than itself, and need not.
